# Two filtered layers of a convolution chain: spectrum, lag convolution and way back merged into one program, with one store per spectrum row block

## What is computed

```python
x = x + L0(_gn(x))   # filtered: rfft2 to 256x256, a 16x16 matrix per frequency, back
x = x + L1(_gn(x))   # patch mixer with big weights (Wq, Wk, Wv, Wout)
x = x + L2(_gn(x))   # local 3x3 convolution
x = x + L3(_gn(x))   # filtered again, with its own filters

def filtered(x, h0, numerators, denumerator):
    H_truncated = rfft2(b, s=(128, 128)) / rfft2(a, s=(128, 128))
    H_full = h0 + rfft2(irfft2(H_truncated), s=(256, 256))[0]
    X = rfft2(x, s=(256, 256), axes=(-3, -2))
    Y = einsum('...hwi,ijhw->...hwj', X, H_full)
    return irfft2(Y)[..., :128, :128, :]
```

## Time and profile before

| | us |
|---|---|
| median of 3 runs | 3530.05 (3528.9 to 3532.25) |
| span of the profiled execution | 3535.8 |
| PE busy | 3239.9 (92%) |
| ACT busy | 1681.8 (48%) |
| DVE busy | 1570.7 (44%) |
| POOL busy | 1257.6 (36%) |
| filtered layer L0, from the loads of the image to the last addition | 637.8 to 1178.1 |
| filtered layer L3 | 2996.5 to 3528.9, then the output store to 3535.8 |

### The profile page before, as it was taken

The page is one execution under the profiler, slowest core; times in us unless marked ns, Lnnn a source line. Parts: engine busy times, 40 slices in busy tenths (PEclk is TensorE's granted clock), DMA queues, the critical chain, the costliest instruction groups (busy, mean ns, idle before and its releaser), DMA issues. The chain is left out here.

```text
span 3535.8 us, 82659 instructions
## 1 busy us (share of the span) xinstructions
PE 3239.9 (92%) x37272; PEld 2671.5 (76%) x37272; DVE 1570.7 (44%) x1926; ACT 1681.8 (48%) x1763; POOL 1257.6 (36%) x1018
## 2 busy tenths in 40 slices
PE   7999999589998699999899999999989978799996
PEld 6999998289997576666687776666678754499996
DVE  6788876411111434444765543343764454311111
ACT  3666665356553344444554434444454431455650
POOL 6888885055552102222540001222280000255550
PEclk9999999799999899999999999999999988899998
DMA  0333333877775521222133332121222353867765
GB/s 18 115 120 121 121 115 132 223 210 198 195 191 126 147 95 61 82 72 82 61 108 100 109 113 76 67 95 48 86 81 60 95 157 55 200 193 193 196 184 154
DMA packets 259193, 429.38 MB, mean 121 GB/s; under 512 B 27479, under 2 KB 105817, under 8 KB 257369
## 3 DMA queue, kind: packets, MB, share of 16 engines
q1 hardware_dynamic: 244746, 398.80, 38.8%
q10 hardware_dynamic: 14096, 25.31, 2.2%
HBM read 306.59 MB, written 114.29 MB: 119 GB/s over the span
## 5 line engine op out<-in xcount | busy, mean ns | idle before, releaser
L138 PE MATMUL m_bank<-xn,w 128*128 128x512 f32 x1536 | 618.3, 403 | 31.9 <-DVE m_store L1563 11.7
L139 PE MATMUL m_bank<-xn,w 128*128 128x512 f32 x1536 | 602.5, 392 | 0.0
L140 PE MATMUL m_bank<-xn,w 128*128 128x512 f32 x1536 | 601.9, 392 | 0.0
L802 PE MATMUL c_acc<-c_shifted,filt 128*32 128x224 f32 (+8 forms) x11264 | 455.4, 316 | 30.9 <-DMA c_shifted<-spectrum_dram 27.7
L802 PEld LDWEIGHTS c_acc<-c_shifted,filt 128*32 128x32 f32 x11264 | 441.8, 159 | 38.7 <-DMA c_shifted<-spectrum_dram 29.3
L581 ACT ACTIVATE filt<-filt 64x2048 f32<-64x2048 f32 (+3 forms) x256 | 424.7, 1758 | 20.4 <-PEq L18 11.0
L568 POOL TENSOR_TENSOR filt<-filt 64x1408 f32<-64x1408 f32 x64 | 259.5, 4055 | 486.8 <-DMA filt<-filters_dram 486.8
L129 ACT ACTIVATE w<-raw_weights 128x2048 fp32r<-128x2048 f32 x96 | 372.9, 3884 | 102.8 <-PE m_bank L140 101.5
L138 PEld LDWEIGHTS m_bank<-xn,w 128*128 128x128 f32 x1536 | 290.9, 189 | 173.1 <-issue 76.4
L133 DVE TENSOR_TENSOR w<-raw_weights,w 128x2048 fp32r<-128x2048 f32 x86 | 333.3, 3875 | 159.2 <-ACT w L129 159.2
L140 PEld LDWEIGHTS m_bank<-xn,w 128*128 128x128 f32 x1536 | 290.8, 189 | 62.9
(11 more groups left out here) (179 smaller groups left out, 6766.6 us busy)
## 6 DMA issues: line engine op xcount, KB each, us to landing
c_shifted<-spectrum_dram SPq DMA_DIRECT2D x256, 270.0 KB, 3.9
filters_dram<-f_stage SPq DMA_DIRECT2D x128, 512.0 KB, 3.5
filt<-filters_dram SPq DMA_DIRECT2D x240, 256.0 KB, 4.6
raw_weights<-in_L_conv_Wq SPq DMA_DIRECT2D x16, 2048.0 KB, 8.6
raw_weights<-in_L_conv_Wk SPq DMA_DIRECT2D x16, 2048.0 KB, 8.5
raw_weights<-in_L_conv_Wv SPq DMA_DIRECT2D x16, 2048.0 KB, 8.6
m_qf<-in_L_conv_Wout SPq DMA_DIRECT2D x128, 256.0 KB, 3.8
spectrum_dram<-s_rows SPq DMA_DIRECT2D x128, 136.0 KB, 2.4
```

Source lines behind the costliest of these rows:

```text
L138: pe.matmul(out, w[0], x[0], start=first, stop=False)
L139: pe.matmul(out, w[0], x[1], start=False, stop=False)
L140: return pe.matmul(out, w[1], x[0], start=False, stop=last)
L802: mm = nc.tensor.matmul(acc[k % 2][phase][32 * s:32 * s + 32, 0:B, LAGS * kb:HALF], filt[:, k, phase, :, :, 4 * kb + s].rearrange("p j c - ...
```

## The change

`spectrum`, `convolve` and `back_to_image` become one function `filtered_layer` with one block, so there is one clearing of semaphores and one closing barrier per layer instead of three. Tiles are shared: `rows` is slot 3 of `shifted`, `cols` and the image's banks lie in memory and PSUM of the convolution, `prod` lies over the filters (32 x 512 numbers per partition, in `filt` slots 0 to 2). What it does beyond that:

- The units of the spectrum come in a new order, even parity first with an odd one after every third channel: the 16 even ones are positions 0 to 20, the last 11 are odd.
- A unit is stored by one DMA, from 128 partitions to a pattern of 2 x 64 rows (`row_block`), instead of two.
- SP issues the four row loads of group 0 after position 26, and those of group 1 after the last store, before it waits for the stores. Group 0 can start when its rows have landed, the filters are turned and PE has done the last spectrum matmul.
- The products of groups 0 to 27 are loaded while groups 29 to 31 run: even ones after groups 28 and 29, odd ones after groups 29 and 30 (48 rows a half). Groups 28 to 31 are no longer stored to DRAM; SP copies their results from `out` to `prod` inside SBUF, two DMAs for each group, from 64 partitions to 4.
- PE runs the even halves of the first three units of the way back before it waits for the odd products.
- `inv_w` is loaded at the start of the layer.

```diff
-            for u in range(2 * C):
-                i, par = u // 2, u % 2
-                sp.wait_ge(rows_ready, u + 1)
-                for part in range(2):
-                    sp.dma_start(scratch["spectrum"][part, i, par * FW:(par + 1) * FW],
-                                 rows[part * FW:(part + 1) * FW, u % 4].rearrange("p b q t -> p (b q t)")).then_inc(stored[u % 4], 16)
-            for k in range(4):
-                sp.wait_ge(stored[k], 16 * 2 * (2 * C // 4))
+    ROW_ORDER = []
+    for i in range(C):
+        ROW_ORDER.append((0, i))
+        if i % 3 == 2:
+            ROW_ORDER.append((1, i // 3))
+    ROW_ORDER += [(1, i) for i in range(C // 3, C)]
+    LAST_EVEN = max(v for v, (par, i) in enumerate(ROW_ORDER) if par == 0)
+    FIRST_LOAD_AT = LAST_EVEN + 6
...
+        def row_block(i, par):
+            at = scratch["spectrum"][:, i, par * FW:(par + 1) * FW]
+            return bass.AP(tensor=at.tensor, offset=at.offset, ap=[[C * L * B * ROW, 2], [B * ROW, FW], [1, B * ROW]])
...
+            sp.dma_start(inv_w[:], const["inv_w"]).then_inc(inv_in, 16)
+
+            for v, (par, i) in enumerate(ROW_ORDER):
+                sp.wait_ge(rows_ready, v + 1)
+                sp.dma_start(row_block(i, par), rows[:, v % 4].rearrange("p b q t -> p (b q t)")).then_inc(rows_stored[v % 4], 16)
+                if v == FIRST_LOAD_AT:
+                    for k in range(4):
+                        sp.wait_ge(rows_stored[k], 16 * len(range(k, LAST_EVEN + 1, 4)))
+                    for s in range(4):
+                        load_rows(sp, 0, 0, s)
+            for s in range(4):
+                load_rows(sp, 1, 1, s)
             for k in range(4):
+                sp.wait_ge(rows_stored[k], 16 * (2 * C // 4))
...
+            def load_products(par, freqs, channels, signal):
+                for c in range(2):
+                    sp.dma_start(prod[FW * c + freqs.start:FW * c + freqs.stop, par, channels],
+                                 scratch["products"][FW * par + freqs.start:FW * par + freqs.stop, channels, c]).then_inc(signal, 16)
+
+            def move_products(g):
+                k, f = g % RING, 4 * (g - GROUPS // 2)
+                for c in range(2):
+                    sp.dma_start(prod[FW * c + f:FW * c + f + 4, 1],
+                                 out[c:128:2, k].rearrange("p b t q -> p (b t q)")).then_inc(last_in, 16)
+
+            SETTLED = slice(0, 4 * (LAST_BATCH - GROUPS // 2))
+            sp.wait_ge(progress, POINTS * (LAST_BATCH + 1))
+            for k in range(RING):
+                sp.wait_ge(prod_stored[k], 16 * (N_BATCHES - 1))
+            load_products(0, slice(0, FW), slice(0, 12), even_in)
+            sp.wait_ge(progress, POINTS * (LAST_BATCH + 2))
+            load_products(0, slice(0, FW), slice(12, 16), even_in)
+            load_products(1, SETTLED, slice(0, 8), odd_in)
+            sp.wait_ge(progress, POINTS * (LAST_BATCH + 3))
+            load_products(1, SETTLED, slice(8, 16), odd_in)
+            for k in range(RING):
+                sp.wait_ge(acc_out, LAST_BATCH + k + 1)
+                move_products(LAST_BATCH + k)
...
+            def group(n, k):
+                g = RING * n + k
+                pe.wait_ge(rows_in[k], 64 * (n + 1))
+                if g == 0:
+                    pe.wait_ge(first_turned, 4)
+                    pe.wait_ge(cleared, 4)
+                else:
+                    pe.wait_ge(turned, 2 * g - 1)
+                if g == 1:
+                    pe.wait_ge(rows_ready, 2 * C)
...
+            pe.wait_ge(inv_in, 16)
+            pe.wait_ge(even_in, 16 * 4)
+            pe.wait_ge(acc_out, GROUPS - 1)
+            for u in range(AHEAD):
+                back(u, 0)
+            pe.wait_ge(odd_in, 16 * 4)
+            pe.wait_ge(last_in, 16 * 2 * RING)
+            for u in range(AHEAD):
+                back(u, 1)
+            for u in range(AHEAD, len(UNITS)):
+                if u >= 4:
+                    pe.wait_ge(added, u - 3)
+                back(u, 0)
+                back(u, 1)
...
+            for v in range(2 * C):
+                act.wait_ge(freq_ready, v + 1)
+                if v >= 4:
+                    act.wait_ge(rows_stored[v % 4], 16 * (v // 4))
```

More of the change, by code:

```diff
@@ L582, in lower_columns, with filtered_layer @@
                           scale=1.0 if column else -1.0)
-def spectrum(nc, image, source, layer, filt, scratch, const, tag):
+def filtered_layer(nc, layer, image, source, spare, filt, scratch, const, out_dram, tag):
+    N_BATCHES = GROUPS // RING
+    RUN = B * ROW - LAGS
+    FAR_AT, FAR = 2 * LAGS * NEAR, L - 2 * LAGS * NEAR
+    POINTS, HALVES_DONE = 11, 6
+    SPREAD = (0, 1, 2, 3, 5, 6, 7, 8)
+    LAST_BATCH = RING * (N_BATCHES - 1)
+    QUARTERS = 4
+    UNITS = [(quarter, b) for quarter in range(QUARTERS) for b in range(B)]
+    AHEAD = 3
+    ROW_ORDER = []
[6 more added lines that the diff above has]
+    FIRST_LOAD_AT = LAST_EVEN + 6
+    TURN_AT = {19: (slice(EVEN, SUM), 0), 22: (slice(EVEN, SUM), 1), 25: (slice(SUM, 3), 0), 28: (slice(SUM, 3), 1)}
     with ExitStack() as ctx:
@@ L591, in spectrum @@
         fwd_w = sb("fwd_w", [L, 2, 128])
+        inv_w = sb("inv_w", [128, 2, L])
         eps = sb("eps", [128, 1])
@@ L599, in spectrum @@
         rstd = sb("rstd", [128, 32])
[L600 to L604, removed]
+        shifted = sb("shifted", [128, RING, 4, B, 2, HALF + LAGS])
+        odd = sb("odd", [128, 2, B, 1 + HALF])
+        both = sb("both", [128, 2, B, HALF])
+        rows = shifted[:, RING - 1]
+        cols = spare[:].rearrange("p a r n -> p (a r n)").rearrange("p (i b h) -> p i b h", i=C, b=B)
+        total = spare[:, 0].rearrange("p r n -> p (r n)").rearrange("p (k m t) -> p k m t", k=RING, t=HALF)
+        out = spare[:, 1].rearrange("p r n -> p (r n)")[:, 0:RING * B * L].rearrange("p (k b t q) -> p k b t q", k=RING, b=B, q=2)
+        prod = filt[:].rearrange("p k h j c n -> p (k h j c n)")[:, 0:2 * C * B * L].rearrange("p (o j n) -> p o j n", o=2, j=C)
+        acc = [[ps(f"acc{k}{phase}", [128, 2 * B, HALF]) for phase in range(3)] for k in range(2)]
+        direct = [ps(f"direct{k}", [128, B, FAR + 2]) for k in range(2)]
+        turn = [a[:].rearrange("p (b g) t -> p b (g t)", b=B) for a in (*acc[0], acc[1][2])]
+        freq = [acc[1][k][:].rearrange("p (b g) t -> p b (g t)", b=B) for k in range(2)]
+        tot = direct[1][:].rearrange("p b f -> p (b f)")[:, 0:64]
+        img = [a[:].rearrange("p (j g) t -> p j (g t)", j=4) for a in (*acc[0], acc[1][0])]
         image_in = [sem(f"image_in{b}") for b in range(B)]
@@ new lines, in _, with sum_of_filters @@
+        @block.gpsimd
+        def _(pool):
+            def sum_of_filters(n, k):
+                pool.wait_ge(filt_in[k], 64 * (n + 1))
+                sum_filters(nc.gpsimd, filt, k).then_inc(filt_summed, 1)
+            for k in range(EARLY):
+                sum_of_filters(0, k)
+            pool.wait_ge(freq_ready, 2 * C)
+            for n in range(N_BATCHES):
+                for k in range(RING):
+                    if RING * n + k >= EARLY:
+                        sum_of_filters(n, k)
+                    pool.wait_ge(rows_in[k], 64 * (n + 1))
+                    at = shifted[:, k].rearrange("p s b q t -> p (s b) q t")
+                    nc.gpsimd.tensor_tensor(total[:, k], at[:, :, 0, 0:HALF], at[:, :, 1, 0:HALF], ALU.add).then_inc(rows_summed, 1)
@@ L637, in _ @@
             dve.memset(rows[:, :, :, :, 0:LAGS].rearrange("p k b q t -> p (k b q) t"), 0.0).then_inc(zeroed, 1)
+            nc.vector.memset(odd[:, :, :, 0:1], 0.0).then_inc(edge_set, 1)
             for n in range(32):
```

359 lines of the change are left out of this document (135 added, 224 removed).

## The result

The changed kernel takes **3809.65 us** (median of 4, 3806.43 to 3830.29) where the kernel before takes 3531.15 beside it: 1.0774 times as long, 95% interval 1.0718 to 1.083. The profiled executions span 3804.6 and 3535.8 us, +268.8.

What follows compares the result with a forecast made beforehand. TensorE paces the lag convolution; the seams around it are what can change. Stores 126 + 126, groups 2 and 3 2 x 1, copies 11 + 9, loads 2 x 1.5: +277 us on 3530 gives 3807 us, range 3700 to 3900.

Steps and rivals of the forecast that it cites:

- The store: Spectrum stage: 32 one-DMA stores on two engines at 5.95 us each, 93 ns a packet; entry +126 us per layer.
- The step from the count of completions to the number of engines: Spectrum store: 39 completions left for three 65-row DMAs, 13 each, so engines follow the outermost count; 2 outermost means 2 engines.
- rival 3: Spectrum stores: two engines at 150 ns a packet, +234 us more, about 4030 us; chance 0.05.
- Group 1: Second lag group, after the spectrum stores: 12.3 us plus 2 for a PE coming out of idling.
- Groups 2 and 3: Lag groups whose filters and rows are issued after all stores: 1 us per layer, bounds 0 and 5.
- Part 2 at nothing: Layer entry: one program, even rows first, group 0 loaded early; costed at nothing beyond the store working, uncovered under 1 us.
- rival 1: Stores and copies spread over 16 engines: -18 us per layer at the entry, shorter tail, 3451 us; chance 0.09.
- The loads beside the last groups: Last three groups, product loads beside them: upper bound 3 x 0.5, lower 0; the upper taken, 1.5 us per layer.
- The copies: Tail: eight SBUF copies into 4 partitions, 4.3 us each, last_in about T + 34 (T: last group's addition ends); +11 and +9 us.
- The sign that I named: New profile: forecast wrong if the copies into filt land in under 5 us.
- The tail as a whole: Last groups and products: +1.5 us per layer for load traffic, and +11 and +9 us for the copies.

Runs made afterwards that it cites:

- experiments 1 and 2: 1: changed kernel, stores in two, 3563.0 us; kernel before, new store only, 3814.17. 2: changed kernel, store of 128 equal steps, layers +25.7; as 4 x 32, 3564.67.

## Why the prediction was right

The forecast was 3807 us, in the range 3700 to 3900; 3809.65 was measured. The mechanism was the one forecast, but two terms of the tail were off and made up for each other, which was luck.

**The store.** The step from the count of completions to the number of engines held: 13.1% of the engines, two completions a store, 5.57 us. The packet takes 5.57 / 64 = 87 ns, not 93: the row of the lone product store had the price already, 88 ns, and scaling it with the bytes made it worse. By that the first store's issue to the start of group 1 is 188.7 and 187.9 us, forecast 195.4. (In rival 3 the sum is 3807 + 234 = 4041, not 4030; nothing hangs on it.)

**Group 1** took 19.3 to 19.9 us where I had 14.3. It stands beside the burst for groups 2 and 3 and stops for 2.50 us at "issue". With the store -7, with this +5: +122.9 and +122.4 for +126. Groups 2 and 3: +2.3 and +4.3, in the bounds 0 and 5 of my 1 us.

**Part 2 at nothing** is borne out as far as this goes: with the store undone, the layers are 15.4 us apart from before, and the last groups and products, +12.0 and +16.4, are more than all of it; up to the end of group 3 that kernel is 2.7 and 1.1 us ahead. What rival 1 said the early group 0 would win (18 us a layer) came to 8.4 and 10.4 at the end of group 0 and was mostly gone by group 3. The 16 engines were right for that rival; that the burst would take the gain back it did not see.

**The loads beside the last groups** are the term that was mis-sized: 1.5 us a layer forecast, +24.9 and +23.3 measured. The step that failed took the 0.70 share of the loop as the price of traffic. The share was about the same (0.76); what differed was the transfer, 512 to 1536 KB in place of 256 and 270. No row of before shows such a load beside PE's work, so the upper bound of 3 x 0.5 had no right to be a bound.

**The copies.** +11 and +9 forecast for the products, -7.1 and -12.3 measured. From the first issue (3733.3) to PE's release (3767.9) eight take 34.6 us, 4.3 us each, as forecast, but the price was right by accident: they stand in part behind the loads, and take 2.7 to 3.3 us when free of them. (The sign that I named, copies landing in under 5 us, can't be read: the profile has no landing time for them.) And they began 19 us before the last addition, since the last group itself was stretched; last_in came at T + 15, not T + 34, and PE waited 13 us for it, not 30. The tail as a whole, last groups and products, is +12.6 and +16.2 where I had +10.5 and +12.5: the sum came near only because one mis-sized term hid the other.

**The count of engines.** The rule of the Trainium skill (DMA: Bandwidth & Descriptors, Why a DMA increments its semaphore by 16 and not by 1) agrees with experiments 1 and 2, with the addition that equal steps are merged before they are counted. Its advice for one 128-partition transfer in place of two halves (the same page, Rules for kernel authors) cost 137 us a layer here as the change applied it, and won 3 to 5 at the end of group 0 with a pattern that merges; the same section also says that an outermost count below 16 confines a DMA to at most that many engines, which is what happened here.

## What to carry to other kernels

Before two DMAs are joined into one, look at the outermost count that remains after merging, on both sides: it decides how many engines will carry it (2 for a count of 2, 13 for 65, 16 for 128), and the completions in the DMA view tell it for any DMA of an existing trace. Loads that are moved under a busy PE go in small transfers, let go by its progress: here 256 KB, paced, cost 1.3 and 1.7 us a group (layers 3 and 0) where 768 KB and more cost 6 to 9. A gain at a seam is measured three groups later, since what was brought forward can crowd what follows.

## What the runs showed of the hardware that I had not expected

PE can be stopped for up to 6.5 us by DMA traffic that it doesn't depend on, as "issue" time; over the stretch the DMA share averages 0.74. There were 19.3 us of stops in 62 us, the granted clock fell to 0.86 on average, and PE was busy for some 8 us longer, about 2 of which also appear with the clock at 1.00. A single 768 KB transfer in flight is enough: the next instruction packet started when that load was nearly through, and each stop ended 1.3 to 1.9 us after such a packet landed. A pattern of 4 x 32 equal steps runs on 16 engines. A copy of 32 KB into one SBUF partition lands in 2.8 us when issue leaves room, and in 7.4 us when both queues are full.
